# Layer 0 of a feature-interaction network from four tiles and the squares of the fields, its squares' step on 32 rows of TensorE's array, and the last addition over d on GpSimd

## The chip, the cores and the metric

The kernel runs on one core of a Trainium2 chip. Its engines work side by side, each through its own list of instructions, and wait for each other by semaphores: TensorE (PE, matrix products; its weight loads are PEld), VectorE (DVE), ScalarE (ACT), GpSimd (POOL, which also issues the gathers) and SyncE (SP, which issues the other DMAs). The metric is the device time of one execution in microseconds (us). Three runs of the kernel before took 643.6, 643.84 and 643.71 us, median 643.71.

## The reference

The batch has 1024 samples with 32 fields; each field's row of 16 numbers is gathered from its table. Three layers of outer products follow, then a small tower. All is float32.

```python
e = stack([tbl_f[ids[:, f]] for f in range(32)], axis=1)      # 1024 x 32 x 16
xk, outs = e, []
for W in (W0, W1, W2):                                        # W0: 32 x 32 x 64; W1, W2: 32 x 64 x 64
    xk = relu(einsum('bmd,bhd,mhk->bkd', e, xk, W))
    outs.append(sum(xk, axis=2))                              # over d
h = concatenate([*outs, dense_ctx], axis=1)                   # 1024 x 208
y = relu(relu(h @ W_top1 + b_top1) @ W_top2 + b_top2) @ W_top3
```

In layer 0 both operands are e, so the product of fields m and h stands in the sum twice, with W0[m, h] and W0[h, m]: 32 x 31 / 2 = 496 unordered pairs and 32 squares, 528 products in all.

## The kernel before

The batch is cut into 16 periods (q) of 64 samples. In a period the 16 values of d times 64 samples are the columns: 1024, held as two halves of 512. A period is thus two sub-steps s = 2q and s = 2q + 1 of 512 columns. The loop over slots j = 0..31 runs, in each slot, layer 1 of sub-step j + 1 beside layer 2 of sub-step j - 1.

Layers 1 and 2 of one sub-step are 16 contraction steps each. VectorE makes their operands (`outer`, L482): an instruction multiplies four tiles of `rows` (the fields of e, spread over 128 partitions) by x, 128x2048, and its result goes into one of the five buffers of `prod` (RING). So a slot has eight such instructions, 2 layers x 2 halves x 2 units. TensorE (`outer`, L595) takes two of them at a time: four steps of two matrix products of 128 rows x 64 columns that stand beside each other, one for each layer, into the halves of `acc[j % 2]`. VectorE's instruction n waits with `s_used` until TensorE has taken instruction n - 5.

Layer 0 has five steps a period (LAYER0_TILES, L12): step k multiplies tile k of `rows` by `mates`, a list of fields in an order such that the 5 x 128 products hold all 528; a product that occurs a second time has weight zero. For periods 0 and 1 VectorE makes the products (L479), from period 2 on GpSimd does (L383), into five buffers `prod0` (RING0). TensorE contracts them (`layer0`, L584; `contract`, L572, two matrix products side by side for the two halves of the columns) into `acc0`: from period 2 on three steps after the first unit pair of slot 2q - 2 and two steps after its second (SUM0, L115).

ScalarE applies relu and writes x1, x2 (L739, L745), and z (L751) into `zin12` and `zin3`, sorted so that d is innermost. The sum over d is made in halves: GpSimd adds 8 values to 8, 4 to 4, 2 to 2 (`add_halves`, L386), and VectorE adds the last two (`sum_d`, L502) into `za` (16 times) and `zc` (8 times, for two periods each but the last). `zc` is copied into `zb` by ScalarE (L806).

The fields of a period come so: GpSimd issues 16 gathers two periods ahead (L365); TensorE turns them (`turn_fields`, L560, into `spread`); ScalarE copies them (L734); SyncE writes them to DRAM in the order of the list (L283, five DMAs), reads `mates` back (L291) and then `rows` in two groups of four tiles (L297). Every fourth period or so a stage of the tower is laid between unit pairs (`tower_step`, TOWER_AT, L135): stages 0 and 1 eight matrix products of 256 columns each by L642/L643, stage 2 eight by L647, stage 3 two by L651. Every one of these products appears in the records as two instructions, since the operands are float32.

Orders on all engines are written out in the program; no scheduler chooses them.

Of the kernel before, what the change touches and what calls it, by code (L numbers as in the profile page):

```python
# [11 lines left out]
LAYER0_TILES = (0, 1, 2, 3, 4)  # L12
MATES = 104
# [6 lines left out]
def cin_tower_kernel(nc, dense_t, ids, table, first_row, w_top1, b_top1, w_top2, b_top2, w_top3,  # L20
                     w0_in, w0_swapped_in, w1_in, w2_in, y_out):
# [38 lines left out]
    L0 = len(LAYER0_TILES)  # L60
    RING0 = 5
# [47 lines left out]

    FIELDS_AT = {(0, 3): 2}  # L110
# [40 lines left out]

    def made_before(q, k, vector):
        return sum(on_vector(a) == vector for a in range(q + 1) for b in range(L0) if (a, b) < (q, k))

# [7 lines left out]
    with ExitStack() as ctx:  # L162
# [9 lines left out]
        w0 = sb("w0", [P, L0, HID])  # L172
# [13 lines left out]
        mates = sb("mates", [P, N])  # L186
        prod0 = sb("prod0", [P, RING0, N])
# [9 lines left out]
        h2 = sb("h2", [P, TOP2 // P, 4 * BT])  # L197
# [5 lines left out]
        w0_swapped = h1[:, :, :].rearrange("p m b -> p (m b)")[:, 0:L0 * HID].rearrange("p (t k) -> p t k", k=HID)  # L203
# [17 lines left out]
        s_mates = sem("s_mates")  # L221
# [8 lines left out]
        s_eight, s_four, s_half12, s_half3 = sem("s_eight"), sem("s_four"), sem("s_half12"), sem("s_half3")  # L230
# [7 lines left out]
        def tower_cols(g):  # L238
            first, count = TOWER[g]
            return slice(first * BT, (first + count) * BT)  # L240

# [29 lines left out]
        def _(sp):  # L271
# [43 lines left out]
            sp.dma_start(w0_swapped, w0_swapped_in).then_inc(s_w0, 16)  # L315
            for w, w_in in ((w1, w1_in), (w2, w2_in)):
                sp.dma_start(w[:, :, :], w_in).then_inc(s_w12, 16)
# [34 lines left out]
        def _(pool):  # L352
# [22 lines left out]
            def product0(q, k):  # L375
                t = LAYER0_TILES[k]
                if k == 0:
                    pool.wait_ge(s_mates, (q + 1) * 16)
                for g, (start, _) in enumerate(GROUPS):
                    if t == start:  # L380
                        pool.wait_ge(s_rows[g], q * 16)
# [4 lines left out]
            def add_halves(z, n, done):  # L386
# [5 lines left out]
                nc.gpsimd.tensor_tensor(by_d[:, :, 0:PAIR], by_d[:, :, 0:PAIR], by_d[:, :, PAIR:QUAD], ALU.add).then_inc(done, 1)  # L392
# [3 lines left out]
            def halve12(p):  # L396
                pool.wait_ge(s_z1, p + 1)
                pool.wait_ge(s_z2, 2 * p + 2)
                add_halves(zin12[p % 2][:, :], p + p // 2 + 1, s_half12)

            def halve3(p):
                pool.wait_ge(s_z3, 2 * p + 2)
                if p == LAST - 1:

                    pool.wait_ge(s_half12, PERIODS)
                    add_halves(zin3[third(p), :], PERIODS + p // 2 + 1, s_half3)
                else:
                    add_halves(zin3[:, :], p + p // 2 + 2, s_half3)
# [6 lines left out]
            pool.wait_ge(s_l0, L0)  # L415
# [34 lines left out]
        def _(dve):  # L450
# [9 lines left out]
            dve.wait_ge(s_w0, 32)  # L460
            nc.vector.tensor_tensor(w0[:, :, :], w0[:, :, :], w0_swapped, ALU.add).then_inc(s_w0sum, 1)
# [11 lines left out]
            def product0(q, k):  # L473
                t = LAYER0_TILES[k]
# [3 lines left out]
                wait_for(dve, s_l0, q * L0 + k - RING0 + 1)  # L478
                nc.vector.tensor_tensor(prod0[:, (q * L0 + k) % RING0, :], rows[:, slot(q, t), :], mates[:, :],  # L479
# [26 lines left out]
            def sum12(p):  # L506
                dve.wait_ge(s_half12, p + 1)
                sum_d(za[:, p * BT:(p + 1) * BT], zin12[p % 2], PAIR, s_za)

            def sum3(p):  # L510
                if p < LAST:
                    dve.wait_ge(s_half3, (p + 1) // 2 if p < LAST - 1 else PERIODS // 2)
                if p < LAST - 1:

                    wait_for(dve, s_zb, p - 3)
                    sum_d(zc[p // 2 % 2], zin3, PAIR, s_zc)
                elif p == LAST - 1:
                    wait_for(dve, s_zb, p - 2)
                    sum_d(zc[p // 2 % 2][third(p), :], zin3[third(p), :], PAIR, s_zc)
                else:  # L520

                    s = 2 * p + 1
                    dve.wait_ge(s_used, taken(2, s, 1, UNITS - 1))
                    dve.wait_ge(s_last_four, 1)
                    for c in range(2):
                        wait_for(dve, s_last_add, c)
                        nc.vector.scalar_tensor_tensor(last_sums[:, 0:PART], sums_alone(s)[c * HID:(c + 1) * HID, 0:PART], 0.0,
                                                       last_sums[:, 0:PART], ALU.max, ALU.add).then_inc(s_last_add, 1)
                    dve.wait_ge(s_last_add, 2)
                    nc.vector.tensor_tensor(last_sums[:, 0:2 * BT], last_sums[:, 0:2 * BT], last_sums[:, 2 * BT:PART],  # L530
                                            ALU.add).then_inc(s_last_add, 1)
                    dve.wait_ge(s_last_add, 3)
                    nc.vector.tensor_tensor(zb[0:HID, p * BT:(p + 1) * BT], last_sums[:, 0:BT], last_sums[:, BT:2 * BT],
                                            ALU.add).then_inc(s_zb, 1)

            for k in range(L0):
                product0(0, k)
            for j in range(SUBS):
                for i, unit in enumerate(vector_units(j)):
                    outer(*unit)  # L540
                    if j % 2 == 1:
                        if i == 2 and j > 1:
                            sum12(j // 2 - 1)
                        if i == 5 and j == SUBS - 1:
                            sum12(LAST)
                        if i == 6 and j > 1 and (j % 4 == 1 or j == SUBS - 1):
                            sum3(j // 2 - 1)
                if j == 0:
                    for k in range(L0):
                        product0(1, k)  # L550
            sum3(LAST)
# [7 lines left out]
        def _(pe):  # L559
# [24 lines left out]
            def layer0(k, q):  # L584
                if on_vector(q):
# [7 lines left out]
                contract(acc0, w0[:, k, :], prod0[:, (q * L0 + k) % RING0, :], k == 0, k == L0 - 1).then_inc(s_l0, 1)  # L593
# [330 lines left out]
```

## Time and profile before

| | |
|---|---|
| median of three runs | 643.71 us |
| the profiled execution | 643.61 us, of which its span 641.7 us |
| PE busy | 585.4 us (91%) |
| DVE busy | 584.1 us (91%) |
| POOL busy | 470.4 us (73%) |
| ACT busy | 357.6 us (56%) |
| granted TensorE clock | 1.0 |
| DMA | 96.51 MB, mean 150 GB/s |

The busy time of an engine is the union of its instructions' spans. GpSimd's share leaves out some 0.3 us between two gathers, in which it issues. "Idle before" names whose result ended an idle time. The chain that ended last goes back from the last instruction, at each point to the one that released it; "issue" in it is time for which no releaser is seen.

### The profile page before, as it was taken

How to read it: one execution, taken by the hardware profiler on the slowest of the kernel's cores; microseconds unless marked ns; L12 is line 12 of the kernel's file. 1: busy time of each engine (PE TensorE's matmuls, PEld its weight loads, DVE VectorE, ACT ScalarE, POOL GpSimd, SP SyncE). 2: the span in 40 equal slices, each digit the busy share in tenths (PEclk: the TensorE clock that was granted, in tenths of full speed). 3: DMA queues.
4: the chain of work that ended last, by engine and by line, in shares of the span. 5: the costliest groups of instructions: out<-in, count | busy, mean ns of one | idle time of the engine just before them, and what ended most of it. 6: DMA issues, size and time to landing. Idle time of an engine off the chain costs nothing.

```text
span 641.7 us, 7781 instructions
## 1 busy us (share of the span) xinstructions
PE 585.4 (91%) x2896; PEld 209.3 (33%) x2896; DVE 584.1 (91%) x331; ACT 357.6 (56%) x593; POOL 470.4 (73%) x406
## 2 busy tenths in 40 slices
PE   0078899999898989999999999999999999999998
PEld 0023233232232323333334323333334323334355
DVE  1039899999999999999999999999999999999995
ACT  0006473657556465747666465747676465737551
POOL 6677769698888888888988888888979783803012
DMA  5286596637181735537280826446380926400000
GB/s 162 48 318 150 221 285 169 272 65 298 28 277 64 238 126 127 239 69 294 49 315 6 262 101 181 185 92 272 57 307 4 282 81 183 176 7 2 1 2 1
DMA packets 27138, 96.51 MB, mean 150 GB/s; under 512 B 7414, under 2 KB 12540, under 8 KB 22876
## 3 DMA queue, kind: packets, MB, share of 16 engines
q1 hardware_dynamic: 18908, 93.90, 43.7%
q0 software_dynamic: 8192, 2.11, 2.6%
q8 instruction: 23, 0.38, 0.2%
q14 instruction: 15, 0.12, 0.1%
HBM read 80.25 MB, written 15.73 MB: 150 GB/s over the span
## 4 chain that ended last, share of the span: by engine, by line
DVE 41%; PE 29%; issue 12%; POOL 10%; DMA 5%; SPq 1%; ACT 1%; DVEq 0%; POOLq 0%; ACTq 0%
DVE prod L498 39%; PE acca L604 10%; PE accb L604 9%; POOL emb L365 7%; PE acc L574 3%; DMA rows<-field_dram 3%; POOL prod L383 3%; PE spread L647 2%; DMA field_dram<-zb_field 1%; DVE prod L479 1%; PE accb L625 1%; PE acc L625 1%; SPq L283 1%; PE spread L642 1%; DVE za L503 0%
## 5 line engine op out<-in xcount | busy, mean ns | idle before, releaser
L365 POOL DMA_INDIRECT emb<-in_table,idx x256 | 246.7, 964 | 77.7 <-issue 67.6
L604 PE MATMUL acca<-prod,w 128*64 128x512 f32 x1024 | 229.1, 594 | 2.8 <-DVE prod L498 1.7
L604 PE MATMUL accb<-prod,w 128*64 128x512 f32 x960 | 216.2, 596 | 13.3 <-DVE prod L498 13.3
L383 POOL TENSOR_TENSOR prod<-rows,mates 128x1024 f32<-128x1024 f32 x70 | 164.4, 2381 | 16.8 <-issue 16.4
L498 DVE TENSOR_TENSOR prod<-rows,x1a 128x2048 f32<-128x2048 f32 x64 | 145.7, 2279 | 5.8 <-PE acca L604 3.0
L498 DVE TENSOR_TENSOR prod<-rows,x1b 128x2048 f32<-128x2048 f32 (+1 forms) x65 | 145.8, 2246 | 1.7 <-PE accb L604 1.0
L498 DVE TENSOR_TENSOR prod<-rows,x2a 128x2048 f32<-128x2048 f32 x64 | 145.7, 2279 | 0.8 <-PE accb L604 0.8
L498 DVE TENSOR_TENSOR prod<-rows,x2b 128x2048 f32<-128x2048 f32 x64 | 145.7, 2278 | 0.0
L604 PEld LDWEIGHTS acca<-prod,w 128*64 128x64 f32 x1024 | 71.7, 137 | 144.9 <-issue 133.8
L604 PEld LDWEIGHTS accb<-prod,w 128*64 128x64 f32 x960 | 65.6, 137 | 156.0 <-issue 114.6
L739 ACT ACTIVATE x1a<-acc 64x512 f32<-64x512 f32 x62 | 35.3, 570 | 125.6 <-PE acc L574 124.9
L574 PE MATMUL acc<-prod,w 128*64 128x512 f32 x320 | 75.5, 595 | 3.3 <-DVE prod L479 1.9
L388 POOL TENSOR_TENSOR zin<-zin 128x512 f32<-128x512 f32 (+1 forms) x24 | 30.5, 1270 | 59.9 <-ACT zin L751 59.5
L745 ACT ACTIVATE x1b<-acc 32x512 f32<-32x512 f32 x124 | 69.9, 564 | 5.2 <-DVE prod L498 3.3
L745 ACT ACTIVATE x2b<-acca 32x512 f32<-32x512 f32 x64 | 36.0, 563 | 22.4 <-DVE prod L498 21.7
L751 ACT ACTIVATE zin<-accb 64x512 f32<-64x512 f32 (+1 forms) x32 | 32.9, 1029 | 26.4 <-PE accb L604 23.3
L479 DVE TENSOR_TENSOR prod<-rows,mates 128x1024 f32<-128x1024 f32 x10 | 11.7, 1221 | 39.1 <-DMA rows<-field_dram 37.5
L751 ACT ACTIVATE zin<-acca 64x512 f32<-64x512 f32 x32 | 33.7, 1053 | 15.0 <-PE acca L604 14.6
L574 PEld LDWEIGHTS acc<-prod,w 128*64 128x64 f32 x320 | 22.1, 137 | 51.7 <-issue 39.7
L734 ACT ACTIVATE zb_field<-spread 32x256 f32<-32x256 f32 x64 | 23.9, 374 | 25.1 <-PE spread L568 24.1
L568 PE MATMUL spread<-ident,emb 128*32 128x128 f32 x256 | 11.2, 294 | 26.3 <-DMA emb<-in_table,idx 26.3
L745 ACT ACTIVATE x2b<-accb 32x512 f32<-32x512 f32 x60 | 33.8, 562 | 0.9
(76 smaller groups left out, 258.7 us busy)
## 6 DMA issues: line engine op xcount, KB each, us to landing
rows<-field_dram SPq DMA_DIRECT2D x30, 2048.0 KB
field_dram<-zb_field SPq DMA_DIRECT2D x32, 256.0 KB
mates<-field_dram SPq DMA_DIRECT2D x16, 512.0 KB, 3.8
emb<-in_table,idx POOLq DMA_INDIRECT x256
field_dram<-zb_field SPq DMA_DIRECT2D x32, 128.0 KB
field_dram<-zb_field SPq DMA_DIRECT2D x16, 192.0 KB
rows<-field_dram SPq DMA_DIRECT2D x2, 1024.0 KB, 7.4
rows<-field_dram SPq DMA_DIRECT2D x1, 1536.0 KB, 12.9
```

Of the source, the lines that this page charges most:

```text
L365: pool.indirect_dma_start(out=emb[q % EMBS][:, j * EMB:(j + 1) * EMB], out_offset=None, in_=table, in_offset=bass.IndirectOffsetOnAxis(ap= ...
L383: nc.gpsimd.tensor_tensor(prod0[:, (q * L0 + k) % RING0, :], rows[:, slot(q, t), :], mates[:, :], ALU.mult).then_inc(s_prod0p, 1)
L388: nc.gpsimd.tensor_tensor(by_d[:, :, 0:DH], by_d[:, :, 0:DH], by_d[:, :, DH:EMB], ALU.add).then_inc(s_eight, 1)
L479: nc.vector.tensor_tensor(prod0[:, (q * L0 + k) % RING0, :], rows[:, slot(q, t), :], mates[:, :], ALU.mult).then_inc(s_prod0v, 1)
L498: nc.vector.tensor_tensor(prod[:, n % RING, t:t + count, :], rows[:, at + t:at + t + count, c * HALF:(c + 1) * HALF], xs, ALU.mult).then_i ...
L574: mm = nc.tensor.matmul(to[c * HID:(c + 1) * HID, :], w, operand[:, c * HALF:(c + 1) * HALF], start=first, stop=last)
L604: mm = nc.tensor.matmul(acc[j % 2][side * HID:(side + 1) * HID, :], (w1 if layer == 1 else w2)[:, step, :], prod[:, (made(layer, s, half, ...
L625: mm = nc.tensor.matmul(sums_alone(s)[c * HID:(c + 1) * HID, 0:PART], w2[:, step, :], prod[:, n % RING, i, c * PART:(c + 1) * PART], start ...
L734: last = nc.scalar.activation(by_d[:, d, :, :, :], turned[d * FIELDS:(d + 1) * FIELDS, :, :, :], ACT.Copy)
L739: last = nc.scalar.activation(to[h * HID:(h + 1) * HID, :], src, ACT.Relu)
L745: last = nc.scalar.activation(to[block * FIELDS:(block + 1) * FIELDS, :], src[of:of + FIELDS, :], ACT.Relu)
L751: return nc.scalar.activation(by_d[:, c * count:(c + 1) * count, :], src.rearrange("k (d b) -> k d b", b=BT), ACT.Relu)
```

## The change

From the third period on layer 0 uses 4 x 128 products for the 496 pairs and a separate step for the 32 squares:

- Step 0 multiplies `mates` by `across`, a new tensor of 128 partitions: four blocks of 32 fields, each read by a DMA of its own from the same list in DRAM, shifted by 4, 8, 12 and 16 places. Steps 1 to 3 use tiles 1, 2 and 3 of `rows`. GpSimd makes four products a period, into a ring of four buffers.
- The squares: SyncE reads the 32 fields into a tensor `squares` of 64 partitions x 512 (upper and lower 32 partitions hold the two halves of the columns), ScalarE squares it in place with one instruction, and TensorE contracts it with two matrix products of 32 rows x 64 columns. The order of a period's steps is 0, 1, 2, squares, 3; their number stays five.
- Periods 0 and 1 keep five tiles (EARLY_TILES), with four buffers where there were five. Their weights for tiles 0 and 4 come by a further DMA into h1's place and are added up by a second VectorE instruction at the start.
- `add_halves` gets a fourth instruction on GpSimd, which adds the last two values and writes `za` or `zc`; VectorE's 24 reductions go.
- h2, the tower's second layer, lies in h1, which frees the room for `across`.

```diff
-LAYER0_TILES = (0, 1, 2, 3, 4)
-MATES = 104
+LAYER0_TILES = (1, 2, 3)
+EARLY_TILES = (0, 1, 2, 3, 4)
+MATES, FIELDS_LISTED = 104, 32
+def across_of(q):
+    return field_of(MATES + q % FIELDS_LISTED + 4 * (q // FIELDS_LISTED + 1))
...
-        SUM0[2 * q - 2, 1] = [(k, q) for k in range(3, L0)]
+        SUM0[2 * q - 2, 1] = [(SQUARES, q), (L0 - 1, q)]
...
 def mates_in(q):
                 sp.dma_start(mates[:, :], part).then_inc(s_mates, 16)
+                if q < EARLY_PERIODS:
+                    return
+                for b in range(BLOCKS):
+                    at = q % LISTS * LENGTH + MATES + 4 * (b + 1)
+                    part = bass.AP(field_dram.tensor, at * N, [[N, FIELDS], [1, N]])
+                    sp.dma_start(across[b * FIELDS:(b + 1) * FIELDS, :], part).then_inc(s_across, 16)
+
+            def fields_in(q):
+                wait_for(sp, s_l0, q * STEPS0)
+                for c in range(2):
+                    at = (q % LISTS * LENGTH + MATES) * N + c * HALF
+                    part = bass.AP(field_dram.tensor, at, [[N, FIELDS], [1, HALF]])
+                    sp.dma_start(squares[c * FIELDS:(c + 1) * FIELDS, :], part).then_inc(s_fields_in, 16)
...
                 list_fields(q)
                 mates_in(q)
+                if q >= EARLY_PERIODS:
+                    fields_in(q)
                 for g in range(len(GROUPS)):
                     rows_in(q, g)
...
 GpSimd, product0
-                wait_for(pool, s_l0, q * L0 + k - RING0 + 1)
-                nc.gpsimd.tensor_tensor(prod0[:, (q * L0 + k) % RING0, :], rows[:, slot(q, t), :], mates[:, :],
-                                        ALU.mult).then_inc(s_prod0p, 1)
+                pool.wait_ge(s_l0, q * STEPS0 if q == EARLY_PERIODS else summed_before(q - 1, k) + 1)
+                other = across[:, :] if k == 0 else rows[:, slot(q, LAYER0_TILES[k - 1]), :]
+                nc.gpsimd.tensor_tensor(prod0[:, k, :], other, mates[:, :], ALU.mult).then_inc(s_prod0p, 1)
 GpSimd, add_halves
-                nc.gpsimd.tensor_tensor(by_d[:, :, 0:PAIR], by_d[:, :, 0:PAIR], by_d[:, :, PAIR:QUAD], ALU.add).then_inc(done, 1)
+                nc.gpsimd.tensor_tensor(by_d[:, :, 0:PAIR], by_d[:, :, 0:PAIR], by_d[:, :, PAIR:QUAD], ALU.add).then_inc(s_pair, 1)
+                pool.wait_ge(s_pair, n)
+                nc.gpsimd.tensor_tensor(to, by_d[:, :, 0], by_d[:, :, 1], ALU.add).then_inc(done, 1)
...
 VectorE
-            def sum_d(to, z, count, done):
-                nc.vector.tensor_reduce(to[:, :], z[:, :].rearrange("k (b d) -> k b d", d=EMB)[:, :, 0:count],
-                                        mybir.AxisListType.X, ALU.add).then_inc(done, 1)
...
             for j in range(SUBS):
-                for i, unit in enumerate(vector_units(j)):
+                for unit in vector_units(j):
                     outer(*unit)
-                    if j % 2 == 1:
-                        if i == 2 and j > 1:
-                            sum12(j // 2 - 1)
...
 TensorE, layer0
+                if k == SQUARES and not on_vector(q):
+                    pe.wait_ge(s_squares, q + 1 - EARLY_PERIODS)
+                    for c in range(2):
+                        part = slice(c * FIELDS, (c + 1) * FIELDS)
+                        mm = nc.tensor.matmul(acc0[c * HID:(c + 1) * HID, :], w0[part, SQUARES, :], squares[part, :],
+                                              start=False, stop=False)
+                    mm.then_inc(s_l0, 1)
+                    return
...
 ScalarE
+            def square_fields(q):
+                act.wait_ge(s_fields_in, (q + 1 - EARLY_PERIODS) * 2 * 16)
+                nc.scalar.activation(squares[:, :], squares[:, :], ACT.Square).then_inc(s_squares, 1)
...
                 if j < SUBS - 2:
+                    if j % 2 == 0:
+                        square_fields(j // 2 + 1)
                     input1(j + 2, 0)
```

Three places show how the lists move. On GpSimd, in period 3 (prod0 are layer 0's products, emb1 the gathered rows, zin121 and zin3 the z of layers 0 and 1 and of layer 2), there stood before:

```order
L383 TENSOR_TENSOR prod0<-rows,mates 128x1024 [waits s_l0,s_rows0,s_mates]
L383 TENSOR_TENSOR prod0<-rows,mates 128x1024 [waits s_l0] x2
L365 DMA emb1<-in_table,idx 128x16 [waits s_turned]
L365 DMA emb1<-in_table,idx 128x16 x3
L383 TENSOR_TENSOR prod0<-rows,mates 128x1024 [waits s_l0]
L383 TENSOR_TENSOR prod0<-rows,mates 128x1024 [waits s_l0,s_rows1]
L365 DMA emb1<-in_table,idx 128x16 x4
L388 TENSOR_TENSOR zin121<-zin121 128x64x8 [waits s_z2,s_z1]
L390 TENSOR_TENSOR zin121<-zin121 128x64x4 [waits s_eight]
L392 TENSOR_TENSOR zin121<-zin121 128x64x2 [waits s_four]
```

And now:

```order
L435 TENSOR_TENSOR prod0<-across,mates 128x1024 [waits s_l0,s_across,s_mates]
L435 TENSOR_TENSOR prod0<-rows,mates 128x1024 [waits s_l0,s_rows0]
L435 TENSOR_TENSOR prod0<-rows,mates 128x1024 [waits s_l0]
L417 DMA emb1<-in_table,idx 128x16 [waits s_turned]
L417 DMA emb1<-in_table,idx 128x16 x3
L435 TENSOR_TENSOR prod0<-rows,mates 128x1024 [waits s_l0]
L417 DMA emb1<-in_table,idx 128x16 x4
L439 TENSOR_TENSOR zin121<-zin121 128x64x8 [waits s_z2,s_z1]
L441 TENSOR_TENSOR zin121<-zin121 128x64x4 [waits s_eight]
L443 TENSOR_TENSOR zin121<-zin121 128x64x2 [waits s_four]
L445 TENSOR_TENSOR za<-zin121 128x64 [waits s_pair]
```

The fifth product is gone, the first no longer waits for `rows`, and a small addition stands behind each row of three.

On TensorE, in slot 2q - 2 behind its second unit pair, there stood before (acca gathers layers 1 and 2, acc0 layer 0):

```order
L604 MATMUL acca<-prod,w2 64x512
L574 MATMUL acc0<-prod0,w0 64x512 [waits s_prod0p]
L574 MATMUL acc0<-prod0,w0 64x512
L574 MATMUL acc0<-prod0,w0 64x512 [waits s_prod0p]
L574 MATMUL acc0<-prod0,w0 64x512
L604 MATMUL acca<-prod,w1 64x512 [waits s_prod]
```

And now:

```order
L648 MATMUL acca<-prod,w2 64x512
L619 MATMUL acc0<-squares,w0 64x512 [waits s_squares]
L619 MATMUL acc0<-squares,w0 64x512
L604 MATMUL acc0<-prod0,w0 64x512 [waits s_prod0p]
L604 MATMUL acc0<-prod0,w0 64x512
L648 MATMUL acca<-prod,w1 64x512 [waits s_prod]
```

The number of matrix products is the same; one pair of them uses 32 rows of the array and waits for ScalarE and not for GpSimd.

On SyncE's list, in period 3, `mates` and `rows` stood one behind the other:

```order
L291 DMA mates<-field_dram 128x1024 [waits s_prod0p,s_prod0v,s_listed]
L297 DMA rows<-field_dram 128x4096 [waits s_rows0,s_prod]
L297 DMA rows<-field_dram 128x4096 [waits s_rows1,s_prod]
L283 DMA field_dram<-zb_field 32x4x512 [waits s_prod,s_field]
```

And now:

```order
L326 DMA mates<-field_dram 128x1024 [waits s_prod0p,s_prod0v,s_listed]
L332 DMA across<-field_dram 32x1024 x4
L340 DMA squares<-field_dram 32x512 [waits s_l0]
L340 DMA squares<-field_dram 32x512
L346 DMA rows<-field_dram 128x4096 [waits s_rows0,s_prod]
L346 DMA rows<-field_dram 128x4096 [waits s_rows1,s_prod]
L318 DMA field_dram<-zb_field 32x4x512 [waits s_prod,s_field]
```

Six DMAs and a wait for TensorE's last step of the layer 0 before stand ahead of the two large ones.

## Rows read from the trace of the kernel before

**Rows 1.** Two periods: length, busy PE, PEld, DVE, ACT, POOL (instructions); clock, DMA share, GB/s.
```profile
251.90:287.26 35.36, 34.87 (x174) 12.22 (x172) 35.36 (x18) 22.19 (x36) 30.57 (x26) 1.00 0.50 166
...
322.81:359.80 36.99, 36.50 (x182) 13.73 (x180) 36.63 (x18) 22.23 (x36) 31.73 (x27) 1.00 0.50 159
```

**Rows 2.** DVE's line 503: count, ns min/median/max, first and last start.
```profile
L503 DVE TENSOR_REDUCE za<-zin x16: 274/277/281, 118.9 to 627.3; 128x64 f32<-128x128 f32 x16
L503 DVE TENSOR_REDUCE zc<-zin x8: 276/277/284, 163.5 to 629.8; 128x64 f32<-128x128 f32 x7, 64x64 f32<-64x128 f32 x1
```

**Rows 3.** Timeline of DVE at a reduction: start, us, instruction.
```profile
261.80 0.28 DVE L503 TENSOR_REDUCE za<-zin 128x64 f32<-128x128 f32 x1
261.99 2.28 DVE L498 TENSOR_TENSOR prod<-rows,x1a 128x2048 f32<-128x2048 f32 x1
```

**Rows 4.** The chain that ended last, pieces at the borders of its stretches: start, us, what.
```profile
110.94 3.46 PE acca L604 x16
...
177.07 4.71 POOL prod L383 x2
...
478.44 3.65 PE accb L604 x16
...
504.68 3.46 PE acca L604 x16
...
550.73 3.65 PE accb L604 x16
```

**Rows 5.** The chain from 335 us to 365 us.
```profile
335.23 3.65 PE accb L604 x16
338.89 3.65 PE spread L647 x16
...
350.16 3.58 PE acca L604 x16
353.75 2.58 PE acc L574 x12
...
365.05 3.36 DVE prod L498 x2
```

**Rows 6.** Timeline of PE at 180 us, then of DVE; idle before it in brackets.
```profile
179.90 1.03 PE L574 MATMUL acc<-prod,w 128*64 128x512 f32 x4
181.83 1.08 PE L574 MATMUL acc<-prod,w 128*64 128x512 f32 x4 [0.90 <-POOL prod L383]
...
186.49 2.29 DVE L498 TENSOR_TENSOR prod<-rows,x1a 128x2048 f32<-128x2048 f32 x1 [0.75 <-PE acca L604]
```

**Rows 7.** Timeline of PE, then of DVE, in an undisturbed slot.
```profile
276.86 0.68 PE L568 MATMUL spread<-ident,emb 128*32 128x128 f32 x16
277.51 3.65 PE L604 MATMUL acca<-prod,w 128*64 128x512 f32 x16
...
275.18 2.28 DVE L498 TENSOR_TENSOR prod<-rows,x1a 128x2048 f32<-128x2048 f32 x1
...
292.76 2.28 DVE L498 TENSOR_TENSOR prod<-rows,x1a 128x2048 f32<-128x2048 f32 x1
```

**Rows 8.** GpSimd's third addition, by line and form: busy us, mean ns | idle before.
```profile
L392 POOL TENSOR_TENSOR zin<-zin 128x128 f32<-128x128 f32 x23 | 9.2, 399 | 1.8
```

**Rows 9.** Timeline of ACT in an undisturbed slot, at x1a.
```profile
324.55 1.15 ACT L739 ACTIVATE x1a<-acc 64x512 f32<-64x512 f32 x2 [6.98 <-PE acc L574]
```

**Rows 10.** Timeline of SP, POOL and PE, period 2; then of SP, POOL, period 8.
```profile
86.72 0.93 SPq L297 DMA_DIRECT2D rows<-field_dram  x2
...
95.99 11.72 POOL L383 TENSOR_TENSOR prod<-rows,mates 128x1024 f32<-128x1024 f32 x5 [3.37 <-issue]
...
103.05 2.75 PE L574 MATMUL acc<-prod,w 128*64 128x512 f32 x12
...
287.75 1.05 SPq L297 DMA_DIRECT2D rows<-field_dram  x2
...
305.92 7.06 POOL L383 TENSOR_TENSOR prod<-rows,mates 128x1024 f32<-128x1024 f32 x3
```

More of the change, by code:

```diff
@@ L107, in taken @@
         return pairs_of(j, half, u) if j < SUBS - 1 else made(layer, s, half, u) - pairs_of(j, 0, 0) + 1
+    SQUARES = L0
+    ALONE0 = [t for t in EARLY_TILES if t not in LAYER0_TILES]
     FIELDS_AT = {(0, 3): 2}
@@ L150, in on_vector, with products, place0, order0 @@
         return q < 2
+    def products(q):
+        return EARLY if on_vector(q) else L0
     def made_before(q, k, vector):
-        return sum(on_vector(a) == vector for a in range(q + 1) for b in range(L0) if (a, b) < (q, k))
+        return sum(on_vector(a) == vector for a in range(q + 1) for b in range(products(a)) if (a, b) < (q, k))
+    def place0(q, k):
+        return (q * EARLY + k if on_vector(q) else k) % RING0
+    def order0(q):
+        return [*range(EARLY)] if on_vector(q) else [*range(L0 - 1), SQUARES, L0 - 1]
+    STEPS0 = EARLY
+    assert STEPS0 == L0 + 1
+    def summed_before(q, k):
+        return q * STEPS0 + order0(q).index(k)
     def slot(q, t):
@@ L537, in _ @@
+            for k in range(EARLY):
                 product0(0, k)
             for j in range(SUBS):
-                for i, unit in enumerate(vector_units(j)):
+                for unit in vector_units(j):
                     outer(*unit)
-                    if j % 2 == 1:
-                        if i == 2 and j > 1:
-                            sum12(j // 2 - 1)
[L544 to L547, printed above, removed]
@@ L548, in _ @@
                 if j == 0:
-                    for k in range(L0):
+                    for k in range(EARLY):
                         product0(1, k)
-            sum3(LAST)
+            last_sum3(LAST)
             dve.wait_ge(s_wide, 32)
@@ L592, in layer0 @@
                     wait_for(pe, s_z1, q)
-                contract(acc0, w0[:, k, :], prod0[:, (q * L0 + k) % RING0, :], k == 0, k == L0 - 1).then_inc(s_l0, 1)
+                if not on_vector(q):
+                    w = w0[:, k, :]
+                elif EARLY_TILES[k] in LAYER0_TILES:
+                    w = w0[:, 1 + LAYER0_TILES.index(EARLY_TILES[k]), :]
+                else:
+                    w = w0_early[:, ALONE0.index(EARLY_TILES[k]), :]
+                contract(acc0, w, prod0[:, place0(q, k), :], k == 0, k == products(q) - 1).then_inc(s_l0, 1)
             def outer(j, half, u):
@@ L689, in _ @@
             keep_busy(acc[1][:, :], 5)
-            pe.wait_ge(s_w0sum, 1)
-            for k in range(L0):
+            pe.wait_ge(s_w0sum, 2)
+            for k in order0(0):
                 layer0(k, 0)
@@ L705, in _ @@
                     if (j, i) == (0, 2 * UNITS - 1):
-                        for k in range(L0):
+                        for k in order0(1):
                             layer0(k, 1)
@@ L821, in tower_step @@
                     for j in range(TOP2 // P):
-                        done = nc.scalar.activation(h2[:, j, 0:width], tower[:, j * width:(j + 1) * width], ACT.Relu,
+                        done = nc.scalar.activation(h2_of(g)[:, j, :], tower[:, j * width:(j + 1) * width], ACT.Relu,
                                                     bias=b2[:, j:j + 1])
@@ L901, with pairs, tile @@
     w0 = np.asarray(given.pop("L0_rec_W0"))
-    given["w0"], given["w0_swapped"] = np.zeros((2, 128, len(LAYER0_TILES), w0.shape[2]), w0.dtype)
-    seen = set()
-    for k, tile in enumerate(LAYER0_TILES):
-        for q in range(128):
-            a, b = field_of(q + MATES), m[q, tile]
-            if (a, b) not in seen:
-                given["w0"][q, k] = w0[a, b]
-                if a != b:
-                    given["w0_swapped"][q, k] = w0[b, a]
-                seen |= {(a, b), (b, a)}
-    assert len(seen) == w0.shape[0] * w0.shape[1]
+    def pairs(operands):
+        direct, swapped = np.zeros((2, 128, len(operands), w0.shape[2]), w0.dtype)
+        seen = set()
+        for k, other in enumerate(operands):
+            for q in range(128):
+                a, b = field_of(q + MATES), other(q)
+                if (a, b) not in seen:
+                    direct[q, k] = w0[a, b]
+                    if a != b:
+                        swapped[q, k] = w0[b, a]
+                    seen |= {(a, b), (b, a)}
+        return direct, swapped, seen
+    def tile(t):
+        return lambda q: m[q, t]
+    early = [t for t in EARLY_TILES if t not in LAYER0_TILES]
+    direct, swapped, seen = pairs([tile(t) for t in (*LAYER0_TILES, *early)])
+    assert len(seen) == w0.shape[0] * w0.shape[1]
+    n = len(LAYER0_TILES)
+    given["w0_early"] = np.concatenate([direct[:, n:], swapped[:, n:]], axis=1)
+    direct, swapped, seen = pairs([across_of] + [tile(t) for t in LAYER0_TILES])
+    squares = np.zeros((128, 1, w0.shape[2]), w0.dtype)
+    for n in range(FIELDS_LISTED):
+        a = field_of(MATES + n)
+        assert (a, a) not in seen
+        squares[n, 0] = squares[FIELDS_LISTED + n, 0] = w0[a, a]
+    assert len(seen) == w0.shape[0] * (w0.shape[1] - 1)
+    given["w0"], given["w0_swapped"] = np.concatenate([direct, squares], axis=1), swapped
     arrays, aps = {}, {}
```

105 lines of the change are left out of this document (52 added, 53 removed).

## The prediction

> **What bounds the kernel now.** I read the busy times, then the chain of waits, then the timelines where the chain changes engine, then single periods. PE and DVE are both busy 91% of the span, so the average says little. In a usual period (the first of [rows 1]) DVE is busy for the whole 35.36 us: 16 products and a reduction. PE is busy 34.87 us of it. DVE sets the pace and PE follows half a microsecond behind. In a period with the tower's stage 2 (the second of [rows 1]) PE is busy 36.50 of 36.99 us and DVE idles. The chain [rows 4, 5] goes in stretches, of which the rows show the borders: PE up to 114 us, GpSimd to 182, DVE to 335, PE to 365, DVE to 478, PE to 508, DVE to 550.7, PE to the end. GpSimd is really late once [rows 6]: PE's last step of layer 0 begins at 181.83, 0.90 us after PE had run dry, and DVE then idles 0.75 us for PE.
>
> **The change part by part.**
>
> *VectorE's reductions.* There are 24 [rows 2], 13 for za and 6 for zc before 550 us, one za a period and one zc every other. One costs DVE 0.19 to 0.20 us (261.80 to 261.99, [rows 3]); its 0.28 us overlaps the next. By stretch: 3 before 186 us, 7 from there to 335, 6 from 365 to 478, 3 from 508 to 550: 19 where DVE is on the path, 19 x 0.195 = 3.7 us. The other 5 fall where PE bounds and give nothing. Were all of them to count, 24 x 0.195 = 4.7 is the upper end.
>
> *GpSimd.* The fifth product goes: 11.72 / 5 = 2.34 us a period [rows 10]. The fourth addition comes: the third takes 399 ns for 128 columns with 1.8 / 23 = 0.08 us of gap [rows 8], so the fourth, half as wide, 0.48 us at most, 1.5 times a period. That is at least 2.34 - 0.72 = 1.6 us a period net in GpSimd's favour, more than its 0.90 us of lateness: the 0.75 us of DVE's idle time at 186 us goes. za and zc were written by DVE behind GpSimd's third addition, at a fixed place in its list; now they are ready 0.5 us after it, so ScalarE's waits for them are met earlier, not later. Gain 0.75 us; below it 0, if DVE is late at 186 us for its own sake, and nothing above.
>
> *TensorE.* The steps stay five. The squares' pair replaces a pair of the same 512 columns; a step lasts 2.58 / 3 = 0.86 us, one pair of records side by side 0.43 [rows 5]. No row shows 32 rows of the array instead of 128. I take the columns to set the time, so the step itself costs 0.86 as before. What is new is the change of tile shape on the way in and out. The trace has such changes by columns: 16 instructions of 256 columns take 3.65 us [rows 5] where 16 x 0.215 = 3.43 would do, 0.22 over; the sixteen turning products at 276.86 take 0.65 [rows 7] where four abreast need 0.43, again 0.22. I take x = 0.2 us a period. Ends: at 0 nothing is lost. If the array must run empty on each side, an instruction's tail counts: four instructions take 1.03 us [rows 6], 0.43 + 0.60, a tail of 0.17, twice is 0.33. If the two halves also run one behind the other, x is 0.86 more.
>
> What does x cost? While PE bounds, x itself: this is so in four of the fourteen squares' steps, which stand 1.7 us ahead of the pieces at 110.94 and 504.68 [rows 4], in the same place of the stretch in [rows 5], and in period 15 behind 550.7: 4 x 0.2 = 0.8 us. In the other ten DVE bounds, and PE's lateness must first use up a cushion. From the first pair of such a slot PE needs as long as from 350.16 to 365.05 [rows 5], 14.89 us, so it would be done at 277.51 + 14.89 = 292.40 [rows 7]; DVE's instruction that waits for it starts at 292.76. The late product gives the same: the step could have begun at 179.90 + 0.86 = 180.76, came 1.07 us late and cost DVE 0.75, so 0.32 was swallowed [rows 6]. The cushion is 0.3 us; x = 0.2 stays within it. The whole period agrees, barely: DVE needs 35.36 - 0.19 = 35.17, PE 34.87 + 0.2 = 35.07.
>
> A page speaks against this. The Trainium skill, "TensorEngine Tiling (Array Packing)", section Key Properties, says that a change of the tiling mode, other than a change of tile within one, drains TensorE. By the row above a shape change costs 0.22 us for both sides; a full drain would make it 0.33 and the sum 0.9 us worse (4 x 0.13, and 10 x 0.03). The column changes in this trace are such changes too and show 0.22, so I stay with them.
>
> *ScalarE.* One more instruction of 64x512, 0.57 us like half of x1a's pair (1.15, [rows 9]), right before x1a. ScalarE sits idle 6.98 us there, waiting for the very step that needs the squares. It stands at some 317.6 us, PE's squares' step at 322.6. Cost 0; without the cover 0.57.
>
> *SyncE and the DMAs.* Six more DMAs, 0.5 us each to issue (1.05 / 2, [rows 10]), and the wait for the last step of the layer 0 before stand ahead of `rows`. In period 8 rows go out at 287.75 and GpSimd's first product starts at 305.92, 18 us later; two or three of them are given up at no cost. Only period 2 is tight: rows go out at 86.72, GpSimd, idle before it, starts at 95.99, so 2 MB and what went with them took 9.3 us. Now they leave 2 to 3 us later with 0.75 MB more ahead of them, at that rate up to 3.4 us: they are there between 98 and 102. The first product needs none of them; the third then ends between 98 + 4.7 and 102 + 4.7, and PE wants it at 103.05 + 2 x 0.86 = 104.8, in a stretch where PE bounds. Cost 0 to 1.9 us. I take 0: the rate counts other traffic as well, and the nearer end has 2 us to spare.
>
> *Start and end.* The fifth early product now waits for one step of PE given five products before; if that is not hidden, it costs a product of one period. At the end, where PE is on the path from 550.7 on, GpSimd's two sums take 0.5 us longer each and DVE is rid of three reductions. Cost 0, at most 0.5.
>
> **Sum.** 3.7 + 0.75 - 0.8 = 3.65 us gained. The profiled execution took 643.61 us, 0.1 below the median; 643.61 - 3.65 = 639.96. I say 640.0.
>
> **The rivals.**
>
> *A, no net change: the squares' step costs about half a microsecond.* If the array runs empty on three sides, also between the two halves that lie in different rows, x = 3 x 0.165 = 0.5. Then four times 0.5, and ten times 0.5 - 0.3: 2.0 + 2.0 = 4.0 lost against 4.45 gained, 643.2 us. For it: PE has only 0.3 us a period, and no row shows different array rows side by side. Against: the shape changes by columns cost 0.2 in all. Late rows in period 2 (up to 1.9) lead to the same region.
>
> *B, slower: the two halves run one behind the other.* x = 0.2 + 0.86 = 1.06. Each of ten periods loses 1.06 - 0.3 = 0.76, and the four in PE's stretches 1.06: 7.6 + 4.2 = 11.8 against 4.45, so 643.61 + 7.4 = 651 us. It decides from x = 0.6 on: 2.4 + 3.0 = 5.4 against 4.45. For it: half the width that makes a pair fast is lost. Against: in all pairs of the trace different columns are enough for both to run at once. The Trainium skill, "TensorEngine Tiling (Array Packing)", section Gotcha 1: PSUM Pressure, says that different row tiles cannot use the same PSUM bank simultaneously; here both halves write acc0, in different partitions. By that rule taken literally the sum would be this one; no row of the trace bears on it.
>
> *C, faster still: the 32-row step is cheaper than a full one.* If it took 0.43 us of PE, PE's four stretches would be shorter by 4 x (0.43 - 0.2) instead of longer by 0.8: 643.61 - 4.45 - 0.9 = 638.3. Nothing speaks for it but that the step does a quarter of the work.
>
> **How the numbers follow.** The forecast (x from 0 to 0.35, 639.1 to 641) 0.62; A and what lies between, 641 to 644.9, 0.19; B 0.10; C 0.09. Own range of the forecast 639.1 to 641.2. The range that holds 8 in 10: leave out B and the lower half of C, from 638.3 to 644.0. A measurement of this kernel tells 0.2%, 1.3 us, from no change. Faster than that means below 642.4: forecast, C and a third of A, 0.77. Within: 0.12. Slower: B and a rest, 0.11.
>
> **What would show it.** DVE: no instruction of the old line 503, periods of 35.16 us between 190 and 335 us, no idle time at 186. PE: a squares' step of two pairs at once, 0.86 us, and some 0.2 us over in its slot's second layer 0 piece (1.7 becomes 1.9). The PE stretch at 359 us is longer by x. GpSimd: four products, no PE wait for it after 140 us. It would be wrong if DVE showed an idle time in every even slot behind the squares, with PE as releaser: then x is over the cushion, and its length tells whether A or B holds. Rival C would show as a second piece of layer 0 shorter than 1.7 us.

## The result, and the profile after

The changed kernel takes 640.37 us (median of five runs, 639.88 to 641.52) against 643.71 before (five runs, 643.53 to 644.01). The ratio is 0.9951 with a 95% interval of [0.9936, 0.9965]: 3.3 us faster. The forecast was 640.0. The profiled execution, the fastest of the five, took 639.88 us, 3.73 less than that of before; by the medians it is 3.34, and the sum of the steps had said 3.65.

From the page of after:

```profile
span 638.1 us, 7867 instructions
PE 587.9 (92%) x2896; PEld 206.8 (32%) x2896; DVE 579.6 (91%) x308; ACT 366.4 (57%) x607; POOL 446.5 (70%) x416
PE 58%; DVE 25%; issue 7%; DMA 5%; POOL 2%; SPq 1%; ACT 1%; DVEq 0%; ACTq 0%
```

DVE lost 4.5 us of busy time and GpSimd 24 us; PE gained 2.5 us with the same 2896 instructions. The last row is the share of the chain that ended last: PE's share has gone from 29% to 58%. DVE's work still fills a whole period, but PE's does now too. Three periods, with the columns of [rows 1]: one without a stage of the tower, one with a stage of eight products, like the first of [rows 1], and one with stage 2, like its second:

```profile
208.34:243.52 35.18, 33.54 (x167) 10.53 (x165) 35.18 (x17) 22.02 (x38) 27.79 (x27) 1.00 0.60 185
...
279.06:314.23 35.17, 35.15 (x174) 12.03 (x172) 35.17 (x17) 22.91 (x39) 26.92 (x27) 1.00 0.61 185
314.23:351.08 36.85, 36.84 (x182) 13.57 (x180) 36.78 (x18) 23.12 (x39) 31.67 (x28) 1.00 0.58 178
```

A usual period takes 35.17 to 35.18 us, 0.19 less than the 35.36 before: the reduction. In the second of these periods PE is busy 35.15 of 35.17 us, so both engines are full. With stage 2 it is 36.85 where it had been 36.99.

Where does PE's extra time come from? The chain through one slot of layer 0, which answers to [rows 5]:

```profile
310.77 3.63 PE acca L648 x16
314.40 2.58 PE acc L604 x12
316.98 3.43 PE acca L648 x16
320.41 1.00 PE acc L619 x4
321.41 1.01 PE acc L604 x4
322.42 6.87 PE acca L648 x32
```

The second piece of layer 0, squares (L619) and last step (L604), takes 1.00 + 1.01 = 2.01 us, where two ordinary steps took 1.72. So x, the price of the step in another shape, is 0.29 us and not the 0.2 that I took; the upper end had been 0.33.

The weight loads (PEld) at this place show how it looks from inside. A pass is a pair of instructions side by side, 0.43 us for 512 columns, and an ordinary step has two:

```profile
319.38 0.14 PEld L648 LDWEIGHTS acca<-prod,w 128*64 128x64 f32 x2 [0.28 <-issue]
320.34 0.19 PEld L619 LDWEIGHTS acc<-squares,w 32*64 32x64 f32 x4 [0.81 <-issue]
321.34 0.20 PEld L604 LDWEIGHTS acc<-prod,w 128*64 128x64 f32 x4 [0.81 <-issue]
321.83 0.14 PEld L648 LDWEIGHTS acca<-prod,w 128*64 128x64 f32 x2 [0.29 <-DVE prod L554]
322.26 0.14 PEld L648 LDWEIGHTS acca<-prod,w 128*64 128x64 f32 x2 [0.29 <-issue]
```

In a row of like steps there is a load at the start of every pass, 0.43 us ahead of the pass that uses it. On the way into the other shape and on the way out no load runs for 0.81 us, and the next one begins only with its own product (320.34, 321.34). From 319.38 to 322.26 are 2.88 us for six passes, which would take 2.58: 0.30 over. Whether the late load is what costs the time, or only goes with it, the trace doesn't tell.

Where PE bounds, DVE's idle time shows it: the 0.77 us at 365 us have become

```profile
357.31 2.29 DVE L554 TENSOR_TENSOR prod<-rows,x1b 128x2048 f32<-128x2048 f32 x1 [0.29 <-PE acca L648]
...
362.85 2.29 DVE L554 TENSOR_TENSOR prod<-rows,x1a 128x2048 f32<-128x2048 f32 x1 [1.06 <-PE acca L648]
```

1.06 us, 0.29 more. At 186 us, where DVE had idled 0.75 us behind GpSimd's late product [rows 6], it runs through:

```profile
182.73 2.28 DVE L554 TENSOR_TENSOR prod<-rows,x2a 128x2048 f32<-128x2048 f32 x1
184.93 2.29 DVE L554 TENSOR_TENSOR prod<-rows,x1a 128x2048 f32<-128x2048 f32 x1
187.14 2.28 DVE L554 TENSOR_TENSOR prod<-rows,x2a 128x2048 f32<-128x2048 f32 x1
```

The other engines did as costed. ScalarE squares in 0.63 us and then still idles 6.46 us before x1a; GpSimd's fourth addition takes 0.30 us; SyncE sends rows at 288.71, 9.65 us after the start of that period's layer 0 on PE (279.06), where it had been 6.75 us (287.75 [rows 10] after 281.00), so 2.9 us later; in period 2 GpSimd waits 2.65 us for them, and PE starts its layer 0 at 102.81 without a wait for GpSimd. Timelines of after, one for each of the four:

```profile
315.44 0.63 ACT L874 ACTIVATE squares<-squares 64x512 f32<-64x512 f32 x1
322.53 1.15 ACT L783 ACTIVATE x1a<-acc 64x512 f32<-64x512 f32 x2 [6.46 <-PE acc L604]
...
150.68 0.30 POOL L445 TENSOR_TENSOR za<-zin 128x64 f32<-128x64 f32 x1
...
288.71 0.84 SPq L346 DMA_DIRECT2D rows<-field_dram  x2
...
99.11 7.06 POOL L435 TENSOR_TENSOR prod<-rows,mates 128x1024 f32<-128x1024 f32 x3 [2.65 <-DMA rows<-field_dram]
```

Where the time came from can be read off by one landmark, the start of each period's layer 0 on PE, in both traces:

| layer 0 of period | before, us | after, us | after minus before |
|---|---|---|---|
| 2 | 103.05 | 102.81 | -0.24 |
| 3 | 138.12 | 137.99 | -0.13 |
| 4 | 173.89 | 173.16 | -0.73 |
| 5 | 210.09 | 208.34 | -1.75 |
| 6 | 245.64 | 243.52 | -2.12 |
| 7 | 281.00 | 279.06 | -1.94 |
| 8 | 316.55 | 314.23 | -2.32 |
| 9 | 353.57 | 351.08 | -2.49 |
| 10 | 388.84 | 386.26 | -2.58 |
| 11 | 424.20 | 421.44 | -2.76 |
| 12 | 459.75 | 456.61 | -3.14 |
| 13 | 496.78 | 493.46 | -3.32 |
| 14 | 532.05 | 528.64 | -3.41 |
| 15 | 568.68 | 565.09 | -3.59 |
| last piece of layer 2 | 626.95 | 623.66 | -3.29 |

From period 4 on the steps are of three sizes: -0.2 or -0.4 in each period for one or two reductions, about -0.8 between 4 and 5 for GpSimd's late product (beside one reduction), and +0.3 where PE bounds (9 to 10 and 13 to 14, each beside two reductions' -0.4, and after 15 alone). From 2 to 4 it is -0.49 in all, where three reductions and one squares' step where PE bounds would give -0.30; the rest of 0.19 I can't name. One step was not foreseen: between 6 and 7 the lead shrinks by 0.18 although a reduction went, so 0.36 to 0.38 us were lost there, once. The rows of after at that place, of DVE and then of PE:

```profile
253.09 2.28 DVE L554 TENSOR_TENSOR prod<-rows,x2a 128x2048 f32<-128x2048 f32 x1
255.65 2.29 DVE L554 TENSOR_TENSOR prod<-rows,x1a 128x2048 f32<-128x2048 f32 x1 [0.29 <-issue]
...
251.54 7.04 PE L648 MATMUL acca<-prod,w 128*64 128x512 f32 x32
...
262.39 3.65 PE L648 MATMUL accb<-prod,w 128*64 128x512 f32 x16 [0.38 <-DVE prod L554]
```

DVE's instruction at 255.65 starts 0.36 us later than its like: 12.13 us after the start of the period's layer 0 on PE, where it is 11.77 in periods 5 and 7 (220.11, 290.83). PE's piece ahead of it is not late: 251.54 is 8.02 us after that start, as 216.36 and 287.08 are. So the profile names no releaser for the idle time, and PE, which waits for DVE behind it, is not the cause by these rows.

### The profile page after: what moved, and what is told of

Its sections match the earlier page's. It is cut to its first block, busy times and chain, and to the rows that moved or that the text cites. A ratio compares the mean times of both kernels' runs of the same rounds, so it can differ in the third digit from the quotient of the medians.

```text
span 638.1 us, 7867 instructions
## 1 busy us (share of the span) xinstructions
PE 587.9 (92%) x2896; PEld 206.8 (32%) x2896; DVE 579.6 (91%) x308; ACT 366.4 (57%) x607; POOL 446.5 (70%) x416
## 4 chain that ended last, share of the span: by engine, by line
PE 58%; DVE 25%; issue 7%; DMA 5%; POOL 2%; SPq 1%; ACT 1%; DVEq 0%; ACTq 0%
DVE prod L554 24%; PE acca L648 22%; PE accb L648 19%; PE acc L604 6%; DMA rows<-field_dram 3%; POOL emb L417 2%; PE spread L691 2%; PE acc L619 2%; DMA field_dram<-zb_field 1%; PE spread L686 1%; PE accb L669 1%; PE acc L669 1%; PE spread L687 1%; PE spread L598 1%; SPq L318 1%
## 5 line engine op out<-in xcount | busy, mean ns | idle before, releaser
L435 POOL TENSOR_TENSOR prod<-rows,mates 128x1024 f32<-128x1024 f32 x42 | 99.3, 2385 | 6.3 <-DMA rows<-field_dram 6.1
L604 PE MATMUL acc<-prod,w 128*64 128x512 f32 x248 | 59.5, 599 | 0.7 <-DVE prod L535 0.6
L435 POOL TENSOR_TENSOR prod<-across,mates 128x1024 f32<-128x1024 f32 x14 | 33.3, 2381 | 12.8 <-issue 12.6
```

What stands on the lines that cost most here:

```text
L435: nc.gpsimd.tensor_tensor(prod0[:, k, :], other, mates[:, :], ALU.mult).then_inc(s_prod0p, 1)
L604: mm = nc.tensor.matmul(to[c * HID:(c + 1) * HID, :], w, operand[:, c * HALF:(c + 1) * HALF], start=first, stop=last)
```

## The experiments

The experiments ran on three chips, e1 to e3 on one, e5 to e8 on a second, e9 on a third. On all three every kernel takes some 6 to 10 us longer than where the result was taken, the kernel before 8 to 10; the traces show it ahead of 115 us (e5's layer 0 of period 2 starts at 111.13, the changed kernel's on the first chip at 102.81, and the distances behind are alike). So each kernel is compared with the kernel before on the same chip, and by a distance that begins behind that stretch: from the start of period 2's layer 0 to the start of the last piece of layer 2 (103.05 to 626.95 in the table above). The kernel before has a trace on the first chip only; e5 shows that the distance carries over, 520.90 against 520.85 us.

| kernel | median, us | kernel before, us | ratio, 95% interval | distance, us |
|---|---|---|---|---|
| before | | | | 523.90 |
| changed (first chip) | 640.37 | 643.71 | 0.9951 [0.9936, 0.9965] | 520.85 |
| e5, changed again | 647.74 | 651.75 | 0.9937 [0.9915, 0.9958] | 520.90 |
| e1, fourth addition alone | 653.86 | 652.06 | 1.0033 [1.0012, 1.0054] | 525.18 |
| e2, layer 0 alone | 652.07 | 652.06 | 0.9999 [0.9988, 1.0011] | 524.20 |
| e3, squares on 128 rows | 646.80 | 652.06 | 0.9913 [0.9899, 0.9927] | 519.20 |
| e6, the same again | 646.15 | 651.75 | 0.9914 [0.9891, 0.9936] | 519.21 |
| e7, changed and an extra pair | 654.58 | 651.75 | 1.0040 [1.0017, 1.0063] | 526.95 |
| e8, 128 rows and an extra pair | 650.21 | 651.75 | 0.9967 [0.9946, 0.9989] | 522.42 |
| e9, squares on 64 rows | 650.02 | 653.75 | 0.9933 [0.9913, 0.9953] | see below |

### The two parts of the change alone

e1 is the kernel before with this, and VectorE's 24 reductions out:

```diff
-                nc.gpsimd.tensor_tensor(by_d[:, :, 0:PAIR], by_d[:, :, 0:PAIR], by_d[:, :, PAIR:QUAD], ALU.add).then_inc(done, 1)
+                nc.gpsimd.tensor_tensor(by_d[:, :, 0:PAIR], by_d[:, :, 0:PAIR], by_d[:, :, PAIR:QUAD], ALU.add).then_inc(s_pair, 1)
+                pool.wait_ge(s_pair, n)
+                nc.gpsimd.tensor_tensor(to, by_d[:, :, 0], by_d[:, :, 1], ALU.add).then_inc(done, 1)
```

> Before, with the fourth addition on GpSimd alone: VectorE's reductions go, layer 0 keeps five products a period. Theory (three engines were nearly level, and the two parts of the change need each other): VectorE sheds 0.195 us a reduction, but GpSimd gets 0.30 us and a gap of 0.06 more 1.5 times a period, 0.54 us, and already ran level with the others (its fifth product ended 0 to 4 us before it was needed, 1.3 us at 465 us). It becomes the pace: some ten periods x 0.54 = 5.4 us, less 1.3 of slack, less 0.8 that VectorE gains behind the last late product: about 647 us, PE waits for GpSimd's products in many slots. Rival (VectorE's instructions alone set the pace, GpSimd had room): 643.7 - 3.7 = 640.0, no waits for GpSimd.

Measured: slower, 1.0033 of the kernel before, 1.8 us by the medians and 1.3 us by the distance. The direction is the theory's and excludes the rival; the size is a third of what I expected. The waits in total (engine line, released by, us, times, longest), and the worst place on PE and on DVE:

```profile
PEld acc L552 <- POOL prod L383: 15.5, 16, 2.1
...
193.53 1.08 PE L552 MATMUL acc<-prod,w 128*64 128x512 f32 x4 [1.23 <-POOL prod L383]
...
198.19 2.29 DVE L502 TENSOR_TENSOR prod<-rows,x1a 128x2048 f32<-128x2048 f32 x1 [1.89 <-PE acca L582]
```

PE waits for GpSimd's products in 16 places instead of 6 (4.2 us before), and DVE then idles in five slots, 0.64, 1.89, 1.04, 1.06 and 0.89 us, 5.5 us in all where it had been 0.75. Less the 19 reductions' 3.7 us, that is 5.5 - 0.75 - 3.7 = +1.1, near the 1.3. My 647 failed because it subtracted only 0.8 us for the reductions, as if those ahead of the last late product were lost; GpSimd is late in single slots, not all along. This sum was made afterwards.

e2 is the changed kernel with the reductions back on VectorE and three additions on GpSimd, the reverse of the diff above.

> After, with VectorE's reductions kept and GpSimd's fourth addition left out: the change of layer 0 alone. Theory: it removes GpSimd's lateness at 181 us (0.75 us gained) and adds the change of shape, 0.30 us in each of four squares' steps in TensorE's stretches (1.2 us lost), and nothing in the other ten: 643.7 - 0.75 + 1.2 = 644.2 us, between 643.7 and 644.6. Rival (the gain comes from layer 0, by freeing GpSimd and not by VectorE's reductions): 640 to 641.

Measured: 0.9999 [0.9988, 1.0011], no change; the distance is 0.30 us longer, where the theory had 0.5. DVE no longer idles at 186 us (0.75 gained), and x is lost where PE bounds. So neither part is worth anything alone. GpSimd could take over the last addition at a gain only once it had lost a product.

### The shape of the squares' step

e3 and e6 are one kernel: `squares` has 128 partitions with zeros below row 63, and each half has weights that are zero outside its own 32 rows. Both matrix products then have their neighbours' shape.

```diff
-                        part = slice(c * FIELDS, (c + 1) * FIELDS)
-                        mm = nc.tensor.matmul(acc0[c * HID:(c + 1) * HID, :], w0[part, SQUARES, :], squares[part, :],
+                        mm = nc.tensor.matmul(acc0[c * HID:(c + 1) * HID, :], w0[:, SQUARES + c, :], squares[:, :],
```

> After, with the squares' step on all 128 rows: squares is a tensor of 128 partitions whose lower 64 rows of data are followed by zeros, and each half has weights of its own with zeros in the other rows, so that both matrix products have the shape of their neighbours. Theory (0.30 us a squares' step is the change of the array's shape): the second piece of layer 0 falls from 2.02 to 1.72 us, four of them lie where TensorE bounds, and 0.15 us more at 255 us: 640.4 - 1.3 = 639.1 us. Rival (the extra time is the wait for ScalarE's square or the weights' load, not the shape): 640.4, and the piece stays at 2.0.

> The squares' step on all 128 rows, again, now beside the changed kernel. Theory (0.30 us is the change of shape): 1.3 us faster than the changed kernel (four squares' steps of 0.30 and a little), piece 1.72 us. Rival (ScalarE's square or the load): level with it.

> The changed kernel itself, beside the ones that follow: 0.995 of the kernel before, its squares' piece (squares and last step) 2.02 us, and TensorE and VectorE level at 35.17 us a period. Rival (the 0.5% was a matter of the first chip): 1.000.

Measured: e5 gives the change again on another chip, 0.9937 [0.9915, 0.9958], which leaves out 1.000, with usual periods of 35.18 us. e6 took 646.15 against e5's 647.74, run side by side, 1.6 us less; the distances are 519.21 and 520.90, 1.7 us less, and e3 gives 519.20 on its own. The chain through the same slot in e6:

```profile
317.39 3.63 PE acca L648 x16
321.02 2.58 PE acc L605 x12
323.59 3.43 PE acca L648 x16
327.03 0.86 PE acc L619 x4
327.88 0.86 PE acc L605 x4
328.74 6.87 PE acca L648 x32
```

The piece is 1.72 us. ScalarE's square and its wait are still there, so that rival falls: the 0.29 us goes with the shape. The other half of the rival, the weights' load, is not told apart by this run, since the load got its neighbours' shape too; in e6 the loads run 0.43 us apart through the squares' step, as everywhere. The gain is 1.7 us where I expected 1.3. Four times 0.29 is 1.16; the rest is a place that I had put down as 0.15: between the layer 0 of periods 6 and 7, e5 takes 35.54 us and e6 35.16. That is the unforeseen step of the table, 0.38 us. That it comes from the shape is not shown: the kernels that have it (the changed one, e5, e7, e9) and those that don't (e3, e6, e8) differ in the shape, but also by one instruction at the start of VectorE's list, which sets the zeros.

e9 puts both halves in the same 64 rows, with the same sort of padded weights, so that the rows don't change from one half to the other but the shape still differs from the neighbours':

```diff
-                        mm = nc.tensor.matmul(acc0[c * HID:(c + 1) * HID, :], w0[part, SQUARES, :], squares[part, :],
+                        mm = nc.tensor.matmul(acc0[c * HID:(c + 1) * HID, :], w0[0:2 * FIELDS, SQUARES + c, :], squares[:, :],
```

> After, with the squares' step on 64 rows for both halves: the tensor squares keeps its 64 partitions, and each half has weights of its own, zero in the other half's 32 rows, so both matrix products stand in the same rows and no rows change between them; the shape still differs from the neighbours' 128 rows. Theory (the 0.30 us is the change of shape on the way in and out): second piece of layer 0 2.02 us, first layer 0 to the last layer 2 piece 520.9 us as in the changed kernel. Rival (part of the 0.30 us is the change of rows between the two halves): piece 1.9 us or less, 520.4.

Its profiled execution was disturbed between 100 and 160 us (a period of 42 us), so the whole distance says nothing; behind it, from period 3's layer 0 to period 15's, it needs 427.16 us, the changed kernel 427.10 and e6 426.04. PE's timeline there:

```profile
407.45 3.60 PE L647 MATMUL acca<-prod,w 128*64 128x512 f32 x16
410.98 1.08 PE L618 MATMUL acc<-squares,w 64*64 64x512 f32 x4
411.99 1.08 PE L604 MATMUL acc<-prod,w 128*64 128x512 f32 x4
412.89 3.60 PE L647 MATMUL acca<-prod,w 128*64 128x512 f32 x16
```

From 407.45 to 412.89 are 5.44 us, and in the changed kernel as many (316.81 to 322.25); in e6 they are 5.15 (253.09 to 258.24). The rival falls as far as 64 rows tell: with both halves in the same rows the price is the same. Both halves in the same 32 rows (planned as e4) gave no time, since the wider tensor that this takes has no room in SBUF beside the rest.

### The cushion

e7 and e8 add to the changed kernel, and to that with 128 rows, one contraction of 256 columns ahead of a period's first:

```diff
+                if k == 0 and not on_vector(q):
+                    for c in range(2):
+                        nc.tensor.matmul(acc0[c * HID:(c + 1) * HID, 0:PART], w,
+                                         prod0[:, place0(q, k), c * HALF:c * HALF + PART], start=True, stop=True)
```

> The changed kernel with the first half of the first product of each period's layer 0 contracted twice (one more pair of 256 columns from period 2 on, whose result the next pair overwrites): 0.215 us more for TensorE, fourteen times. Theory (VectorE and TensorE are level in every slot of layer 0, the cushion of 0.3 us is used up by the change of shape): each one counts, 14 x 0.215 = 3.0 us slower than the changed kernel. Rival (TensorE still has room in the ten slots in which VectorE bounds): 4 x 0.215 = 0.9 us slower.

> The same extra pair in the kernel whose squares' step has all 128 rows. Theory (without the change of shape the cushion of 0.3 us is there and swallows 0.215 in ten slots): 0.9 us slower than the 128-row kernel, about level with the changed kernel. Rival (no cushion): 3.0 us slower than the 128-row kernel.

Measured: e7's distance is 6.05 us over e5's, e8's 3.21 over e6's, twice and three times the expectations. The size of the added piece was mine to get wrong: a step of 512 columns takes 0.86 us, since each product is two passes, so 256 columns take 0.43 and not 0.215. With 0.43, put in afterwards, the theories give 14 x 0.43 = 6.0 for e7, and 4 x 0.43 + 10 x (0.43 - 0.28) = 3.2 for e8 with a cushion of 0.28. Both fit; the rivals, put right in the same way, would give 4 x 0.43 = 1.7 for e7 and 6.0 for e8, and don't. One usual slot of e7:

```profile
408.06 2.28 DVE L554 TENSOR_TENSOR prod<-rows,x2a 128x2048 f32<-128x2048 f32 x1
410.69 2.29 DVE L554 TENSOR_TENSOR prod<-rows,x1a 128x2048 f32<-128x2048 f32 x1 [0.35 <-PE acca L652]
```

and its period, then e8's:

```profile
398.49:434.10 35.61, 35.59 (x178) 12.32 (x176) 35.26 (x17) 23.02 (x38) 30.57 (x27) 1.00 0.62 184
```

```profile
396.04:431.35 35.31, 35.29 (x178) 12.51 (x176) 35.25 (x17) 23.03 (x38) 30.27 (x27) 1.00 0.60 186
```

35.18 + 0.43 = 35.61 in e7: all of PE's added time counts once the change of shape is in. 35.17 + 0.14 in e8: 0.29 of the 0.43 disappeared.

## Why the prediction was right, point by point

- *VectorE's reductions, 3.7 us on the path.* Right. Between the layer 0 of periods 10 and 15 the lead grows from 2.58 to 3.59 us, 1.0, for seven reductions (7 x 0.195 = 1.37) less one squares' step of 0.29 in PE's stretch; a usual period is 35.17 as worked out.
- *GpSimd's late product, 0.75 us.* Right: the idle time is gone after and in e2, and returns larger in e1. That GpSimd had to shed the product for the additions to be free is shown by e1; the prediction had only noted that the net was in its favour.
- *TensorE, x = 0.2 us.* The mis-sized term: the runs showed 0.29, in the sum four times 0.09, 0.4 us. I had argued from changes of shape by columns, 0.22 us for the two sides, and had 0.33, two full tails, as the end. The 0.22 was a wrong reading. It is what the piece in the other shape itself takes too long; a part of the price stands in the pieces on either side, as the loads of before at the tower's stage 2 show:

```profile
337.86 0.14 PEld L604 LDWEIGHTS accb<-prod,w 128*64 128x64 f32 x2 [0.29 <-issue]
338.82 3.32 PEld L647 LDWEIGHTS spread<-h,t 128*128 128x128 f32 x16 [0.81 <-issue]
342.47 0.20 PEld L604 LDWEIGHTS accb<-prod,w 128*64 128x64 f32 x4 [0.33 <-issue]
...
343.38 0.14 PEld L604 LDWEIGHTS accb<-prod,w 128*64 128x64 f32 x2 [0.29 <-issue]
```

  From 337.86 to 343.38 are 5.52 us for four passes of 0.43 and sixteen of 0.215, 5.16 in all: 0.36 over, in the same count that gives 0.30 for the squares. Read so, the rows of before would have told of a price at or over the cushion. The Trainium skill, "TensorEngine Tiling (Array Packing)", section Key Properties, says that changing the tiling mode drains TensorE; with 0.29 the measurement is nearer to the 0.33 that I had given for that reading than to the 0.2 that I chose. (What I said 0.33 would cost is 4 x 0.13 + 10 x 0.03 = 0.82 us, not 0.9.)
- *The cushion of 0.3 us.* Right, 0.28 to 0.29 by e8. x used it up to the last hundredth, so ten slots stayed free but for the one place below.
- *The whole period, "barely".* DVE needs 35.17 us and PE 34.87 + 0.29 = 35.16, and the periods are 35.17 to 35.18: level, as said. A loss that the sum lacked is the 0.36 to 0.38 us at 255 us, once. Its cause stays open. That the tower's work fills PE from there on does not explain it: the idle time stands ten us ahead of the tower's first stage (265.97), and PE idles 0.38 us behind it.
- *Rival B, the halves one behind the other,* did not occur: the four instructions of the squares take 1.07 us in the timeline, as two pairs. What the Trainium skill, "TensorEngine Tiling (Array Packing)", section Gotcha 1: PSUM Pressure, says of row tiles and a PSUM bank did not show as a delay here, with the two halves in different partitions of acc0. *Rival A* would have needed x = 0.5. *Rival C* falls: the squares' part of the piece takes 1.00 us, and the ordinary step behind it 1.01.
- *ScalarE and the DMAs, 0.* Right; period 2's rows were late for GpSimd by 2.65 us and early enough for PE. (The six DMAs of a period carry 0.66 MB, not the 0.75 of the prediction.)
- *Start and end, 0.* Not met, in our favour: 0.24 us lie ahead of period 2, and PE's last product ends the lead at 3.29 (639.21 to 635.92), so 0.31 us of the span's 3.6 come behind it and 0.13 outside the span. No run shows a reason.

The sum by the measured sizes: 3.7 + 0.75 - 4 x 0.29 - 0.36 = 2.9 us; the landmarks show 3.05 from period 2 on. The prediction's two errors, 0.4 and 0.4 us, were mostly covered by what came at the start and the end, 0.7 us together. So the mechanism was right, and that the number was met to a few tenths is in part luck.

e6 is faster than both kernels: 0.9914 of the one before, against 0.9937 for the changed one beside it. The intervals overlap, but 519.21 and 519.20 against 520.90 and 520.85 us in four traces do not.

## What to carry to other kernels

Where three engines are full to within half a microsecond a period, a part moved from one to the next pays only if the receiver has been relieved as well: e1 lost and e2 gained nothing, together they gave 3.3 us. A small step in a shape of its own is not cheap because it is small: here zeros in the unused rows cost nothing, the change of shape 0.29 us. The price of such a change is read from a start well ahead of it to a start well behind it, and not from the length of the piece alone, which gave 0.22 for 0.36. And a slack that is measured from the trace (here twice, by a late product and by the length of a piece) is worth writing down, since it says up to which price an edit is free.

## What the runs showed of the hardware

A step of 512 columns in 32 rows (the changed kernel) or in 64 rows (e9) of the array, between steps in 128, took 0.29 us more than the same step padded with zeros to 128 rows (e6), on its two sides together: 5.44 against 5.15 us from the piece ahead of it to the piece behind. No run has several steps of 32 or 64 rows in a row, so what one takes there is not shown. A change of the columns alone, by the same count, cost 0.36 us (before, 337.86 to 343.38). In both cases the weight load, which otherwise starts 0.43 us ahead of the pass that uses it, started only with its product.
